# Two chained attention layers: half of the transposes of three units per image through DMA moves and 32 x 32 VectorE squares, and a later load of x

## The reference

```python
# layer 0
hn = group_norm(x, gn1_scale, gn1_bias)
qkv = einsum('bchw,oc->bohw', hn, w_qkv) + b_qkv          # 8 heads of 64 channels
q, k, v = split(qkv.reshape(b * 8, 192, 1024), 3, axis=1)
wgt = softmax(einsum('bct,bcs->bts', q * 64**-0.25, k * 64**-0.25), axis=-1)
a = einsum('bts,bcs->bct', wgt, v).reshape(b, 512, 32, 32)
x = x + group_norm(einsum('bchw,oc->bohw', a, w_proj) + b_proj, gn2_scale, gn2_bias)
# layer 1
qkv = einsum('oc,bcn->bon', weight_norm(v_qkv, g_qkv), x)
qkv = qkv / (sqrt(mean(qkv**2, axis=1)) + 1e-4)
q, k, v = split(qkv, 3, axis=1)
attn = softmax(einsum('bci,bcj->bij', q, k) * 512**-0.5, axis=-1)
h = einsum('oc,bcn->bon', weight_norm(v_out, g_out), einsum('bij,bcj->bci', attn, v))
x = (x + h) * 2**-0.5
```

## Time and profile before

| | |
|---|---|
| median of 3 runs | 3416.3 us (3415.55 to 3417.29) |
| the profiled execution | 3414.62 us, its span 3412.8 us |
| TensorE matmul busy | 3374.6 us (99%), 16816 instructions, 4096 of them transposes |
| VectorE busy | 2118.9 us (62%) |
| ScalarE busy | 1831.0 us (54%) |
| GpSimd busy | 1063.5 us (31%) |
| granted TensorE clock | 0.999 |
| DMA | 332.10 MB, mean 97 GB/s |

### The profile page before, as it was taken

The page is one execution under the profiler, slowest core; times in us unless marked ns, Lnnn a source line. Parts: engine busy times, 40 slices in busy tenths (PEclk is TensorE's granted clock), DMA queues, the critical chain, the costliest instruction groups (busy, mean ns, idle before and its releaser), DMA issues.

```text
span 3412.8 us, 51841 instructions
## 1 busy us (share of the span) xinstructions
PE 3374.6 (99%) x16816; PEld 2776.8 (81%) x16816; DVE 2118.9 (62%) x3452; ACT 1831.0 (54%) x3082; POOL 1063.5 (31%) x947
## 2 busy tenths in 40 slices
PE   8999999999999999999999999999999999999999
PEld 4788888888888888888888888888888888888887
DVE  4577456773577735786457854578555784557744
ACT  3577226772278623785237842378333883247822
POOL 1245113442034410454104531145211452114511
PEclk9999999999999999999999999999999999999999
DMA  8512245222543125341153322542224422343212
GB/s 316 167 39 63 93 114 146 54 58 83 139 120 88 38 91 150 88 100 68 50 150 104 82 75 62 155 99 63 82 71 140 100 63 93 83 138 77 62 56 75
DMA packets 109849, 332.10 MB, mean 97 GB/s; under 512 B 21744, under 2 KB 54768, under 8 KB 98800
## 3 DMA queue, kind: packets, MB, share of 16 engines
q1 hardware_dynamic: 109552, 328.45, 33.9%
HBM read 162.68 MB, written 31.49 MB: 57 GB/s over the span
## 4 chain that ended last, share of the span: by engine, by line
PE 90%; DVE 3%; DMA 3%; SPq 1%; ACT 1%; issue 1%; DVEq 0%; POOL 0%
PE big L471 25%; PE ops L590 14%; PE tps L575 13%; PE big L604 13%; PE big L700 7%; PE big L611 5%; PE tps L771 5%; PE ops L771 4%; PE ops L554 3%; DMA ST<-ST 1%; SPq L387 1%; DMA d_m<-PT 1%; DMA d_u<-ST 1%; PE ops L741 0%; DVE ST L1429 0%
## 5 line engine op out<-in xcount | busy, mean ns | idle before, releaser
L1026 POOL TENSOR_SCALAR PB<-PB,small 128x1024 f32<-128x1024 f32 x576 | 648.2, 1126 | 1311.2 <-DVE small L1256 1298.8
L1250 DVE TENSOR_REDUCE small<-big 128x1 f32<-128x1024 f32 x512 | 625.4, 1222 | 90.5 <-PE big L604 87.3
L1261 DVE TENSOR_TENSOR PT<-tps,PT 128x512 fp32r<-128x512 f32 x1024 | 652.9, 680 | 41.9 <-ACT PT L892 41.6
L892 ACT ACTIVATE PT<-tps 128x512 fp32r<-128x512 f32 x1024 | 564.6, 597 | 162.5 <-PE tps L575 159.5
L886 ACT ACTIVATE PB<-big,small 128x1024 f32<-128x1024 f32 x512 | 572.9, 1119 | 98.2 <-DVE small L1250 95.5
L590 PE MATMUL ops<-PT,VT 128*128 128x512 f32 x2048 | 599.2, 414 | 0.0
L604 PE MATMUL big<-ST 128*128 128x512 f32 x2048 | 554.1, 392 | 7.2 <-DMA ST<-ST 7.2
L575 PEld LDWEIGHTS tps<-ident,PB 128*128 128x128 f32 x4096 | 469.7, 140 | 100.9 <-DVE PT L1261 37.7
L575 PE MATMUL tps<-ident,PB 128*128 128x128 f32 x4096 | 546.6, 274 | 3.5 <-DVE PT L1261 2.7
L604 PEld LDWEIGHTS big<-ST 128*128 128x128 f32 x2048 | 382.6, 188 | 95.0 <-issue 9.7
L590 PEld LDWEIGHTS ops<-PT,VT 128*128 128x128 f32 x2048 | 346.1, 189 | 47.4 <-DVE PT L1261 5.0
(11 more groups left out here) (158 smaller groups left out, 4792.5 us busy)
## 6 DMA issues: line engine op xcount, KB each, us to landing
ST<-ST SPq DMA_DIRECT2D x384, 256.0 KB, 5.0
W<-d_qk SPq DMA_DIRECT2D x32, 1024.0 KB, 6.3
W<-PB SPq DMA_DIRECT2D x256, 128.0 KB, 2.4
XA<-in_x SPq DMA_DIRECT2D x8, 2048.0 KB, 7.6
X<-in_x SPq DMA_DIRECT2D x8, 2048.0 KB, 10.5
W<-d_wp SPq DMA_DIRECT2D x8, 2048.0 KB, 12.0
W<-d_g SPq DMA_DIRECT2D x8, 2048.0 KB, 12.4
W<-d_m SPq DMA_DIRECT2D x8, 2048.0 KB, 7.9
```

What stands on the lines that cost most here:

```text
L892: act_fn(pt_slot(u, s)[:, 0, :], tps[n % 2][:], ACT.Copy).then_inc(s_pt_hi, 1)
L1026: nc.gpsimd.tensor_scalar(PB[:, i, :], PB[:, i, :], rinv[:, i:i + 1], 1.0, ALU.mult, ALU.mult)\
L1250: V.tensor_reduce(negmax[:, i:i + 1], tile(("s", 4 * u + tb))[:], axis=AX.X, op=ALU.max, negate=True).then_inc(s_row_max, 1)
L1261: V.tensor_tensor(pt_slot(u, s)[:, 1, :], tps[n % 2][:], pt_slot(u, s)[:, 0, :].bitcast(f32), ALU.subtract).then_inc(s_pt_ready, 1)
```

## The change

In units 0, 4 and 8 (`MOVED`, the first unit of pairs 0, 1 and 2) the slots 4 to 7, the second 512 keys, are no longer transposed by TensorE.

- The exponential of a moved unit writes its keys interleaved: key s * 128 + k of a half goes to place 4k + s. The transposes of slots 0 to 3 therefore read every fourth element.
- SP issues 16 transfers (`move_quarters`) after the unit's fourth normalised row, from PB to F0, which is X[:, 0:2]. VectorE turns squares (`square`) from F0 to X[:, 2:4], slots 4 and 5 at the end of step 8 and slots 6 and 7 at the beginning of step 11. ScalarE copies them (`moved_hi`) and VectorE subtracts (`moved_lo`), in steps 9 and 11, into W[1][:, 0:2048]. The value matmuls of slots 4 and 5 stand at the end of step 9, those of slots 6 and 7 at the end of step 11.
- `corr` and `head_out` of the moved unit come at steps 12 and 13 instead of 10 to 12.
- The exponential that overwrites the moved rows of PB, in step 8, waits for the moves.
- X and W[1] are in use until unit 8 is done, so the load of x goes behind `stack_head(b, 3, 0)`, where the load of d_g stood, its scaling to steps 50, 52, 54 and 56 of the batch, and the loads of d_wp and d_g behind `stack_head(b, 3, 1)`.

```diff
+MOVED = [4 * pair for pair in range(PAIRS - 1)]
+MOVED_SLOTS = [8 * u + s for u in MOVED for s in range(4, NT)]
+def moved_unit(step, after):
+    return (step - after) // 4 if step >= after and (step - after) % 4 == 0 and (step - after) // 4 in MOVED else None
...
-X_SCALE_STEPS = (20, 23, 26, 29)
+X_SCALE_STEPS = (50, 52, 54, 56)
...
+                def move_quarters(u):
+                    sp.wait_ge(s_p_norm, b * 72 + 4 * u + 4)
+                    own_wait(sp)
+                    if u:
+                        sp.wait_ge(s_squared, moved_count(b, 8 * (u - 4) + NT - 1))
+                        own_wait(sp)
+                    for tq in range(QUARTERS):
+                        for sq in range(QUARTERS):
+                            sp.dma_start(F0[32 * sq:32 * sq + 32, tq, :, :],
+                                         PB[32 * tq:32 * tq + 32, 0:4, HALF + P * sq:HALF + P * sq + P])\
+                              .then_inc(s_moved, 16)
...
-                sp.dma_start(X[:], src_x(b)).then_inc(s_x_res, 16)
+                move_quarters(0)
...
                 stack_head(b, 1, 0)
-                sp.dma_start(W[1][:].bitcast(f32), d_wp[:]).then_inc(s_ld_wp, 16)
                 stack_head(b, 1, 1)
+                move_quarters(4)
                 stack_head(b, 2, 0)
                 stack_head(b, 2, 1)
+                move_quarters(8)
                 stack_head(b, 3, 0)
+                sp.wait_ge(s_moved_lo, b * len(MOVED_SLOTS) + len(MOVED_SLOTS))
+                own_wait(sp)
+                sp.dma_start(X[:], src_x(b)).then_inc(s_x_res, 16)
+                stack_head(b, 3, 1)
+                sp.dma_start(W[1][:].bitcast(f32), d_wp[:]).then_inc(s_ld_wp, 16)
                 sp.dma_start(W[0][:].bitcast(f32), d_g[:]).then_inc(s_ld_g, 16)
-                stack_head(b, 3, 1)
...
-                    if n >= 0:
+                    if n >= 0 and n not in MOVED_SLOTS:
                         transposes(n // 8, n % 8)
                         transposes(n // 8, n % 8 + 1)
-                    if n > 0:
+                    if n > 0 and n - 2 not in MOVED_SLOTS:
                         values0(n - 2)
                         values0(n - 1)
+                    for s, after in ((4, 9), (6, 11)):
+                        if moved_unit(step, after) is not None:
+                            values0(8 * moved_unit(step, after) + s)
+                            values0(8 * moved_unit(step, after) + s + 1)
...
+                    if u in MOVED:
+                        to = to.rearrange("p (h q r s) -> p h s q r", h=2, q=QUARTERS, s=4)
+                        scores = scores.rearrange("p (h s q r) -> p h s q r", h=2, q=QUARTERS, s=4)
+                    if u - 2 in MOVED and tb == 0:
+                        act.wait_ge(s_moved, (b * len(MOVED) + MOVED.index(u - 2) + 1) * EXCHANGE)
...
+                def square(n):
+                    u, s = n // 8, n % 8
+                    if s == 4:
+                        dve.wait_ge(s_moved, (b * len(MOVED) + MOVED.index(u) + 1) * EXCHANGE)
+                    V.transpose(squared(s).rearrange("p (t q r) -> p t q r", t=KB, q=QUARTERS),
+                                F0.rearrange("p q t (r s) -> p s t q r", s=4)[:, s - 4, :, :, :])\
+                     .then_inc(s_squared, 1)
```

More of the change, by code:

```diff
@@ L231, in build @@
         s_pt_ready = sem("pt_ready")
+        s_moved = sem("moved")
+        s_squared = sem("squared")
+        s_moved_hi = sem("moved_hi")
+        s_moved_lo = sem("moved_lo")
         s_o_full = sem("o_full")
@@ L587, in values0 @@
                         pe.wait_ge(s_v_ready, b * 6 + 6)
-                    pe.wait_ge(s_pt_ready, b * 144 + n + 1)
+                    if n in MOVED_SLOTS:
+                        pe.wait_ge(s_moved_lo, moved_count(b, n))
+                        slot = moved_slot(s)
+                    else:
+                        pe.wait_ge(s_pt_ready, own_count(b, n, UNITS))
+                        slot = pt_slot(u, s)
                     for part in range(2):
-                        last = mm(ops[u % 2][:], VT[:, s, P * (u // 2):P * (u // 2) + P], pt_slot(u, s)[:, part, :],
+                        last = mm(ops[u % 2][:], VT[:, s, P * (u // 2):P * (u // 2) + P], slot[:, part, :],
                                   start=(s == 0 and part == 0), stop=(s == 7 and part == 1))
@@ L916, in body @@
                     u, tb, n = step // 4, step % 4, 2 * (step - LAG)
+                    for s, after in ((4, 9), (6, 11)):
+                        if moved_unit(step, after) is not None:
+                            moved_hi(8 * moved_unit(step, after) + s)
+                            moved_hi(8 * moved_unit(step, after) + s + 1)
                     if qk_part(step) is not None:
                         qk_hi(qk_part(step))
-                    if n >= 0:
+                    if n >= 0 and n not in MOVED_SLOTS:
                         pt_hi(n // 8, n % 8)
                         pt_hi(n // 8, n % 8 + 1)
-                    if tb == 2 and u >= 2:
+                    if tb == 2 and u >= 2 and u - 2 not in MOVED and u - 3 not in MOVED:
                         corr(u - 2, 0)
-                    if tb == 0 and u >= 3:
+                    if tb == 0 and u >= 3 and u - 3 not in MOVED:
                         corr(u - 3, 1)
+                    if moved_unit(step, 12) is not None:
+                        corr(moved_unit(step, 12), 0)
+                    if moved_unit(step, 13) is not None:
+                        corr(moved_unit(step, 13), 1)
+                    if moved_unit(step, 15) is not None:
+                        corr(moved_unit(step, 15) + 1, 0)
                     if step < STEPS0:
@@ L1030, in head_out @@
                     pool.wait_ge(s_corr_done, b * 16 + u + 1)
-                    pool.wait_ge(s_p_norm, b * 72 + min(4 * u + 12, 4 * UNITS0))
+                    pool.wait_ge(s_p_norm, b * 72 + min(4 * u + (14 if u in MOVED else 12), 4 * UNITS0))
                     if u == UNITS0 - 2:
@@ L1055, in body @@
                     normalise(n)
-                    if n % 4 == 3 and n >= 8:
+                    if n % 4 == 3 and n >= 8 and n // 4 - 2 not in MOVED:
                         head_out(n // 4 - 2)
+                    if moved_unit(n, 13) is not None:
+                        head_out(moved_unit(n, 13))
                     if n in X_SCALE_STEPS:
@@ L1269, in body @@
                     u, tb, n = step // 4, step % 4, 2 * (step - LAG)
+                    if moved_unit(step, 11) is not None:
+                        square(8 * moved_unit(step, 11) + 6)
+                        square(8 * moved_unit(step, 11) + 7)
+                    for s, after in ((4, 9), (6, 11)):
+                        if moved_unit(step, after) is not None:
+                            moved_lo(8 * moved_unit(step, after) + s)
+                            moved_lo(8 * moved_unit(step, after) + s + 1)
                     if qk_part(step) is not None:
@@ L1279, in body @@
                         recip((step - 1) // 4, (step - 1) % 4)
-                    if n >= 0:
+                    if n >= 0 and n not in MOVED_SLOTS:
                         pt_lo(n // 8, n % 8)
                         pt_lo(n // 8, n % 8 + 1)
+                    if moved_unit(step, 8) is not None:
+                        square(8 * moved_unit(step, 8) + 4)
+                        square(8 * moved_unit(step, 8) + 5)
                 for half in range(2):
```

38 lines of the change are left out of this document (30 added, 8 removed).

## The result

The changed kernel takes **3454.2 us** (median of 4 runs, 3452.43 to 3455.18) beside 3416.8 us for the kernel before in the same comparison: a ratio of 1.0109, 95% interval 1.0096 to 1.0122. It is slower by 37.4 us. That lies inside the range and on the side held likeliest, but not where the likeliest case (3421) put it.

A forecast was written before the change was run, and what follows sets the result against it. TensorE was taken to bound the kernel, with VectorE as full. Per unit -2.0 + 1.3 + 0.95 = +0.25 us, over 24 units +6, rounded to +5 on the median 3416.3: 3421 us, range 3392 to 3480.

The forecast's parts named there:

- the side held likeliest: Whole kernel: slower than before, chance 0.54, against 0.25 for the same and 0.21 for faster.
- the likeliest case: Whole kernel: transposes saved come back as two waits, strides and moves cost nothing; 3421 us, chance 0.33.
- What bounds, and what is removed: TensorE bounds; transposes removed from steps 7 and 8 (1.76 us) and small waits (0.22) save 2.0 us per unit.
- First wait: Before the query-key tile of step 9, TensorE waits 1.3 us per unit for step 7's exponential to free the bank.
- Second wait: Before the transposes of step 10, TensorE waits 0.95 us per unit for VectorE's two ordinary subtractions, late behind the squares.
- Strided access: Exponential, squares and own transposes of moved units touching every fourth element: priced at nothing, upper bound a doubling.
- that rival: "Strides cost": doubled squares 3455, own transposes 3463 (half 3442), exponentials 3459, all about 3535 us; chance 0.36.
- The exponential's upper bound: Strided exponential of a moved unit doubles to 2.24 us; pair 0 hides it, 16 units x 2.4, +38 us, 3459.
- 2 x 0.7 go straight into the wait of step 10: If squares double, the extra of two per unit lengthens the wait before step 10's transposes: +34 us, 3455.
- the sum: Per moved unit -2.0 + 1.3 + 0.95 = +0.25 us; over 24 units +6 us, rounded to +5.
- Moves and x: Moves at 0.71 us an issue land 1.8 us early in pair 0; x's late load and scaling has 0.4 left: nothing.

The follow-up runs named there:

- the fastest kernel: Changed kernel with plain accesses (GpSimd permutes rows), own slots spread over steps 5 to 8, squares 4 and 5 behind the maximum, partner's copy in step 14: 3382.3 us.
- the added transposes: Eight unused transposes added to step 7 of each moved unit, on the changed kernel with all three accesses plain: 3420.98 us, ratio 1.0013.
- the kernel without strides: Changed kernel with exponentials, squares and own transposes all accessing plainly, not a correct computation: 3421.1 us; complete version, with GpSimd writing permuted rows: 3419.44 us.

## Why the prediction was right or wrong

- **What bounds, and what is removed** (-2.0 us per unit): right in kind. With the waits filled, 35 of the 48 us came back. The other 13 can be named only in part: 8.4 us of idle time before the value matmuls of the fastest kernel.
- **First wait, 1.3 us**: right. Measured 1.36, and 0.1 on the first matmul; the added transposes showed that it holds at least 21 us of free room.
- **Second wait, 0.95 us**: right in place and size for the changed kernel (0.9), but by luck in part. I chained squares of 1.4 us and copies that end 1.2 after the exponential, a near tie. Measured without strides it is 0.48 + 0.2 = 0.7 us, and the copies behind the exponential set it. The strided squares add the missing 0.2.
- **The step that failed: "Strided access ... I take the low end, by those rows."** The rows were of patterns broken in runs of 32 elements; a stride of 16 bytes in every element is another thing. Priced at nothing, it cost 33 us: 26.4 for the exponentials, 4.9 for the squares, 2.0 for the own transposes. This is the whole distance from 3421 to 3454.
- **The sizes within that rival.** None of its three times was right for its reason: 3454 is the sum of three costs below their prices, and that it falls beside 3455 and 3459 is luck. The exponential's upper bound was near (2.1 for 2.24 us), its cost over-stated by half (38 for 26): pair 0, thought to hide it, loses 0.8 us at step 5 in batch 1, pairs 1 and 2 some 1.2 each, for 2.4. The squares' was wrong in its step "2 x 0.7 go straight into the wait of step 10": they run beneath an exponential, and of the 0.78 measured extra 0.2 shows. The transposes' was wrong in taking the instruction's price as a whole: only the weight load grew, and most of it lies under the matmuls. Advanced Engine Details and Errata of the Trainium skill, section SBUF Cachelines, had each strided access pay. The runs agree in direction: +88% on the exponential's elements (0.99 of 1.12 us), +56% on a square (1.09 for 0.70), and the runs of 32 elements pay little or nothing.
- **An unpriced term: the partner's copy from step 14 to 15**, 8 to 9 us. The prediction gave it no cost, nor did it name it. So the agreement of 3421 with the kernel without strides is in part errors that cancel: with the copy in step 14 it takes 3411.3, 6 us less than before where the sum said 6 more. Of these 12 us, 6 are the second wait (0.7 for 0.95). Some 4 more are pair 0, for the sum was read in pair 1 alone. In pair 0 of batch 1 the kernel before has a wait that pair 1 has not, in front of the transposes of step 8, and the change removes it:

```profile
549.87 1.25 PE L575 MATMUL tps<-ident,PB 128*128 128x128 f32 x8 [0.34 <-DVE PT L1261]
```

  The scores in front of it end their turn at 548.46 + 0.92 = 549.38, so TensorE waits 0.49 us, 8 x 0.49 = 4; all transposes of the kernel before idle 2.7 us for VectorE, eight times this bracket. The last 2 us stay open.
- **Moves and x, nothing**: right. The 16 issues take 10.62 us (0.66 each, for 0.71) and land after 2.0; in pair 0 of batch 1 the last is down at about 553.8, and the exponential of step 8 starts at 557.14, released by VectorE:

```profile
541.85 10.62 SPq L438 DMA_DIRECT2D X<-PB  x16
...
557.14 1.12 ACT L953 ACTIVATE PB<-big,small 128x1024 f32<-128x1024 f32 x1 [1.48 <-DVE small L1333]
...
X<-PB SPq DMA_DIRECT2D x384, 64.0 KB, 2.0
```

## What to carry to other kernels

A bound that rests on the nearest row must be near in the thing that is in doubt: rows with runs of 32 elements said nothing of a stride on every element, and the low end deserved no more weight than the high one. Work taken from the bounding engine turns into waits of the same size if it filled a fixed chain (here the four microseconds from scores to a free bank); look what other work can be spread into these gaps before judging the removal, since the same removal, without strides, was worth +3 us or -35 by the order alone. And of an instruction that is merely moved by a step, ask what stands behind it: here an exponential whose sums another engine wanted ahead of its next maximum.

## What the runs showed of the hardware

- ScalarE's exponential of 128x1024 takes 2.1 us when it writes every fourth element (16 bytes apart), 1.12 when it writes them side by side; a second-layer exponential of that size, read from SBUF and written in runs of 32, took 1.245.
- VectorE's transposition of 32x32 squares over 128x512 takes 1.09 us reading with that stride, 0.69 in runs of 32.
- TensorE's weight load of a strided 128x128 tile takes some 0.07 us longer (147 against 140 ns in the mean of 3712, 384 of them strided), and nearly all of it is hidden: 2.0 us in the kernel, which is within the noise.
- GpSimd scales 128x512 in 0.69 us whether it writes in permuted runs of 32 or plainly.
- An issue of 32 x 4 pieces takes SP 0.66 us with pieces of 512 bytes and 0.71 with 1 KB: half the bytes save 7% of it. No run here has another count of pieces.
